# Taking the softmax sums from the context matmuls' 65th row, and dropping drains, in a four-stage model on eight cores

## The chip, the cores and the metric

The kernel runs on all 8 cores of one Trainium2 chip. Each core works on one of the 8 batch rows, 2048 tokens of 1024 values, and no core talks to another. The time is that of the slowest core, in microseconds (us) of the device. A core has TensorE (PE), VectorE (DVE), ScalarE (ACT), GpSimd (POOL) and SyncE (SP), each with a queue that it works through in order; PE writes to PSUM, and weights are loaded into it by instructions of their own (PEld).

## What is computed

Two layers, each an attention part and a feed-forward part with a layer norm behind: a gated recurrence, a ternary feed-forward, an attention with relative positions, and a two-deep local-attention block. The change is mainly in the third:

```python
# 8 x 2048 tokens, 16 heads of 64, R = 64
dist = jnp.clip(idx[None, :] - idx[:, None], -R, R) + R
pe_k = rel_emb_k[dist]
pe_v = rel_emb_v[dist]
score = jnp.einsum('bhqd,bhkd->bhqk', q, k) + jnp.einsum('bhqd,qkd->bhqk', q, pe_k)
attn = jax.nn.softmax(score, axis=-1)
ctx = jnp.einsum('bhqk,bhkd->bhqd', attn, v) + jnp.einsum('bhqk,qkd->bhqd', attn, pe_v)
ctx = jnp.transpose(ctx, (0, 2, 1, 3)).reshape(b, s, d)
x = _layernorm(x + ctx @ W_out + b_out)
```

Beyond a distance of 64 all keys on one side share one row of `rel_emb_v`, so their part of the second sum is that row times the sum of their attention weights. That is why the kernel needs two partial sums for every query: that over the keys far to the left and that over the keys far to the right.

The fourth part (two layers, 8 heads, windows of 512) has an attention over 1024 keys for each window and divides by the softmax's sum in the same way.

## The kernel before

The program is written as one list of instructions for each engine, with semaphores: `p.op(engine, ...)` appends an operation, `p.wait(engine, semaphore, value)` a wait, and `p.drain(engine)` an instruction that lets the engine's own earlier work finish. The order in these lists is written out by hand, and each engine keeps to it. The stages run one after the other: build_load_x, build_block0, build_block1, build_block2, build_block3, build_output_store.

build_block2 is the attention with relative positions. For each of 16 heads (`h`) it first writes query products to memory (L947 to L953, 16 transfers), and then goes through 4 query blocks (`qb`) of 512 queries. I call one of these 64 passes a block. A block has these parts:

- Opening: L979 and L981, two matmuls with one row of zeros as weights, open two rows of sums in PSUM, `pb[0:1, 0:512]` and `pb[0:1, 1536:2048]`.
- 16 key steps (`kt`) of 128 keys. The scores come from up to three kinds of matmul: right of the diagonal band (L1050), in the band (L1044 transposes of loaded products, L1055), and left of it (L1060). The exponent (L1067) is taken by ScalarE for all 512 queries. L1072 multiplies the exponents with the 64 values and a column of ones (`VE[kt]`, 65 columns) into `ctxA`, rows 0 to 63 the context and row 64 the full sum. L1075 and L1078 multiply the far parts of the exponents with one column of ones (`onesbc`), into the two rows of sums. The scores of step kt wait for the exponent of step kt - 2 only; the context matmul waits for that of its own step.
- Closing of the two rows (L1079, L1081), and the part for near keys: transposes, a trip through memory, transposes back, 16 small matmuls into `ctxA` (L1101 to L1153).
- Tail: ScalarE copies the two rows of sums to SBUF (L1160, L1161), TensorE adds their products with the two rows of `rel_emb_v` to `ctxA` (L1165, L1167) and closes it (L1169, token `a_close`). VectorE takes the reciprocal of row 64 (L1173) and rounds it (L1175), TensorE spreads it over 64 partitions (L1177), VectorE copies the context (L1181) and multiplies (L1186, token `hb_tok`). TensorE waits for `hb_tok` before the next block.

build_block3 has, in each of two layers, 32 passes over heads and windows. A pass makes scores for a maximum (L1673, L1678, L1682), sends it through memory (L1688 and two transfers into row 64 of the queries), runs the tail of the pass before (attn_tail: L1606, then L1611, L1613, L1615, L1617, L1621, L1627), and then opens and fills its own scores (L1704, L1716, L1727). Three loops in the stages take squares and sum them by turns of VectorE and TensorE, 64 times each: L841 with L847, L1449 with L1455, L1801 with L1807.

## Time and profile before

| | |
|---|---|
| median of 2 runs (lowest, highest) | 11150.66 us (11142.19, 11159.12) |
| profiled execution | 11150.62 us |
| its span, slowest core (fastest core) | 11149.1 us (10966.6 us) |
| busy, PE / PEld | 5631.9 / 1996.6 us |
| busy, DVE / ACT / POOL | 2748.6 / 1682.2 / 840.8 us |
| mean granted clock of the slowest core | 0.608 |

The span is from the first to the last instruction of a core. Busy times of the engines overlap, so they say what an engine did and not what the time waited for; the chain of work that ended last says that. The granted clock is TensorE's, as a share of full speed (2.4 GHz). Ends of matmuls are modelled, so the distance from one start to the next is the safer measure of what a matmul takes.

### The profile page before, as it was taken

Reading aid. Unit: us, or ns where it says so; the run is one execution under the profiler, and the core shown is the slowest. Engines: PE = TensorE matmul, PEld = TensorE weight load, DVE = VectorE, ACT = ScalarE, POOL = GpSimd, SP = SyncE. Lnnn points to the kernel's source line nnn. Section 1 sums busy time; section 2 is a strip of 40 time slices with the busy share of each in tenths; the row PEclk is TensorE's granted clock in tenths of the full one; section 3 lists DMA queues with packets and bytes.
Section 4 is the critical chain, followed back from the end, with each engine's and each line's share of the span. In section 5 each row is a group of like instructions: output and inputs, shape, how many; then the busy total and the mean of one; then the engine's idle time right before and its main releaser. Section 6 shows DMA issues by size and latency. Waiting matters only on the chain.

```text
span 11149.1 us, 60408 instructions; the slowest of 8 cores (10966.6 to 11149.1 us)
## 1 busy us (share of the span) xinstructions
PE 5631.9 (51%) x19111; PEld 1996.6 (18%) x19111; DVE 2748.6 (25%) x4041; ACT 1682.2 (15%) x3009; POOL 840.8 (8%) x813
## 2 busy tenths in 40 slices
PE   4344444444545544545554546323445962344694
PEld 2111111111111111111111112101112420111241
DVE  5655220000000000000000001263344116333314
ACT  1100102222222222222222221001110100111100
POOL 0000100000000000000000000021111102111010
PEclk7676775555555555555555556655567975556796
DMA  3000221111110111111001111200002320000231
GB/s 53 9 4 0 53 31 33 31 32 35 32 32 22 32 32 35 32 35 32 28 25 32 32 35 46 48 5 0 1 0 22 35 28 0 1 0 5 22 35 60
DMA packets 458427, 285.29 MB, mean 26 GB/s; under 512 B 307482, under 2 KB 403995, under 8 KB 454027
## 3 DMA queue, kind: packets, MB, share of 16 engines
q0 software_dynamic: 222240, 81.89, 6.5%
q1 hardware_dynamic: 162156, 103.56, 3.5%
q10 hardware_dynamic: 73728, 95.98, 2.4%
q8 instruction: 169, 2.77, 0.1%
q14 instruction: 134, 1.10, 0.1%
HBM read 227.39 MB, written 118.96 MB: 31 GB/s over the span
## 4 chain that ended last, share of the span: by engine, by line
PE 44%; DVE 17%; DMA 16%; ACT 12%; issue 6%; SPq 2%; DVEq 1%; POOL 1%; ACTq 1%; POOLq 0%; PEldq 0%
DMA sc_amax<-amaxc 6%; PE pm L1072 6%; ACT xb L1067 6%; DMA sc_qre<-wm 4%; PE pm L1905 3%; PE pb L1926 3%; PE pm L1050 2%; SPq L49 2%; PE pb L1075 2%; PE pm L1060 2%; PE pb L1078 2%; DVE wm L1173 2%; DMA xb<-sc_e 2%; PE pm L1044 2%; PE pm L1420 2%
## 5 line engine op out<-in xcount | busy, mean ns | idle before, releaser
L1173 DVE RECIPROCAL wm<-pm 1x512 f32<-1x512 f32 x64 | 214.5, 3352 | 4738.8 <-PE pm L1169 4738.8
L1067 ACT ACTIVATE xb<-pm 128x512 bf16<-128x512 f32 x1024 | 611.4, 597 | 2554.9 <-PE pm L1060 1665.8
L1072 PE MATMUL pm<-xb,U 128*65 128x512 bf16 x576 | 349.9, 608 | 488.9 <-ACT xb L1067 488.9
L49 POOL DMA_DIRECT2D wj<-sc_qre x128 | 70.5, 553 | 5013.1 <-PE pm L1055 2631.1
L947 PE MATMUL pb<-wj 128*128 128x512 bf16 x256 | 147.2, 588 | 500.4 <-ACT wm L953 446.1
L1138 PE MATMUL pb<-identb,xb 128*128 128x128 bf16 x1024 | 119.4, 309 | 539.2 <-DMA xb<-sc_e 539.2
L1682 DVE TENSOR_REDUCE amaxc<-pm 128x1 f32<-128x640 f32 (+4 forms) x256 | 181.8, 740 | 686.3 <-PE pm L1678 684.6
L1727 ACT ACTIVATE xb<-pb 128x512 bf16<-128x512 f32 x448 | 244.7, 595 | 547.8 <-PE pb L1716 547.3
L1060 PE MATMUL pm<-wj 128*128 128x512 bf16 (+4 forms) x576 | 301.5, 524 | 0.0
L1050 PE MATMUL pm<-qer,wj 128*128 128x512 bf16 (+4 forms) x576 | 299.6, 520 | 0.0
L1078 PE MATMUL pb<-xb,onesbc 128*1 128x512 bf16 (+4 forms) x576 | 287.5, 499 | 0.0
L220 PE MATMUL pm<-xb,wj 128*128 128x512 bf16 x512 | 141.2, 444 | 282.4 <-ACT U L231 260.0
L1075 PE MATMUL pb<-xb,onesbc 128*1 128x512 bf16 (+4 forms) x576 | 282.9, 491 | 0.0
L1072 PE MATMUL pm<-xb 128*65 128x512 bf16 x256 | 155.6, 608 | 215.4 <-ACT xb L1067 215.4
L1704 PE MATMUL pb<-wm,zbuf 1*65 1x512 bf16 x64 | 38.6, 603 | 438.3 <-DMA wj<-sc_amax 436.0
L953 ACT ACTIVATE wm<-pb 128x512 f32<-128x512 f32 x256 | 152.9, 597 | 670.3 <-DMA sc_qre<-wm 499.5
L1905 PE MATMUL pm<-xb,wm 128*128 128x512 bf16 (+1 forms) x704 | 188.4, 392 | 99.4 <-DVE xin L1853 99.4
L1420 PE MATMUL pm<-xb,wm 128*128 128x512 bf16 x384 | 109.4, 411 | 220.6 <-DVE xin L1391 169.9
L1145 ACT ACTIVATE xb<-pb 128x512 bf16<-128x512 bf16 x256 | 132.2, 602 | 553.6 <-PE pb L1138 553.6
L1613 DVE RECIPROCAL wm<-wm 1x512 f32<-1x512 f32 x64 | 213.8, 3341 | 5.1 <-issue 0.4
L1072 PEld LDWEIGHTS pm<-xb,U 128*65 128x65 bf16 x576 | 74.9, 130 | 751.3 <-issue 751.3
L49 POOL DMA_DIRECT2D wm<-l1f_w x152 | 128.1, 850 | 1028.5 <-PE pm L1905 521.5
(433 smaller groups left out, 9420.5 us busy)
## 6 DMA issues: line engine op xcount, KB each, us to landing
sc_qre<-wm ACTq DMA_DIRECT2D x256, 256.0 KB, 2.0
wm<-l1f_w POOLq DMA_DIRECT2D x116, 256.0 KB, 4.2
sc_xspill<-xr SPq DMA_DIRECT2D x16, 1024.0 KB, 13.9
xb<-sc_e SPq DMA_DIRECT2D x128, 128.0 KB, 2.8
xb<-sc_e ACTq DMA_DIRECT2D x128, 128.0 KB, 2.9
wm<-W_qkv POOLq DMA_DIRECT2D x48, 256.0 KB, 4.2
sc_e<-xb ACTq DMA_DIRECT2D x112, 96.0 KB, 2.0
sc_e<-xb SPq DMA_DIRECT2D x112, 96.0 KB, 1.9
```

The lines of the kernel that those rows point to most:

```text
L49: self.on(eng, lambda q, o=out, i=in_, s=sem: q.dma_start(out=o, in_=i).then_inc(s.h, 16))
L1050: q.matmul(o, l, r, start=s1, stop=s2), s_tr)
L1060: q.matmul(o, l, r, start=s1, stop=s2), s_tr)
L1067: q.activation(out=o, in_=i_, func=AF.Exp), s_se)
L1072: q.matmul(o, l, r, start=st, stop=False), s_tr)
L1075: q.matmul(o, onesbc[:], r, start=False, stop=False), s_tr)
L1078: q.matmul(o, onesbc[:], r, start=False, stop=False), s_tr)
L1173: p.op("vector", lambda q: q.reciprocal(out=srow[0:1, 0:512], in_=ctxA[64:65, 0:512]))
L1420: q.matmul(o, l, r, start=st, stop=sp),
L1727: q.activation(out=o, in_=i_, func=AF.Exp), s_se)
L1905: q.matmul(o, l, r, start=st, stop=sp),
L1926: q.matmul(o, l, r, start=st, stop=sp),
```

## The change

In build_block2, L1072, L1075 and L1078 are replaced by up to three matmuls with the 65 columns of `VE[kt]`, each over its part of the 512 queries: far right keys into `ctxC` (a bank of `pb`), the band into `ctxA`, far left keys into `ctxB` (a bank of `pm`). All three tiles are opened with zeros at the start of a block. The sums of the far parts are now row 64 of `ctxB` and `ctxC`. The tail adds three tiles instead of reading one: three operations on the sums before the reciprocal, and for the context a copy on ScalarE and two adds on VectorE before the multiplication. The wait of TensorE for the copy of the block before (`cc_prev`) is dropped.

In build_block3 the copy of the sums before the reciprocal (L1611) is dropped; the reciprocal reads PSUM.

In both, drains of VectorE are dropped in several places: L840, L1388, L1394, L1448, L1520, L1764, L1787, L1800, L1931 and L1976.

```diff
@@ -837,7 +837,6 @@
     for (base, ps) in ((0, pm), (8, pb)):
         for nb in range(NB):
             for dt in range(NDT):
-                p.drain("vector")
                 p.op("vector", lambda q, d=dt, b=base, n=nb: q.tensor_tensor(
                     out=bfull[:, 0:512], in0=qkT[b + d][:, n * 512:(n + 1) * 512],
                     in1=qkT[b + d][:, n * 512:(n + 1) * 512], op=OP.mult), s_ve)
@@ -974,12 +973,10 @@
             qb0 = qb * 512
             p.wait("tensor", s_qe[par], qe_tok)
             ctxA = pm[0:66, 1024:1536]
-            if cc_prev:
-                p.wait("tensor", s_ve, cc_prev)
-            p.op("tensor", lambda q: q.matmul(pb[0:1, 0:512], zbuf[0:1, 0:1], MQS[0:1, 0:512],
-                                              start=True, stop=False), None)
-            p.op("tensor", lambda q: q.matmul(pb[0:1, 1536:2048], zbuf[0:1, 0:1], MQS[0:1, 0:512],
-                                              start=True, stop=False), None)
+            ctxB = pm[0:66, 1536:2048]
+            ctxC = pb[0:66, 0:512]
+            for ctx in (ctxA, ctxB, ctxC):
+                p.op("tensor", lambda q, o=ctx: q.matmul(o, zbuf[0:1, 0:66], MQS[0:1, 0:512], start=True, stop=False), None)
             tchunks = {}
             tlist = []
             for kt in range(NTT):
@@ -1067,19 +1064,20 @@
                      q.activation(out=o, in_=i_, func=AF.Exp), s_se)
                 prev_exp_tok[pp] = p.sems["s_se"].n
                 p.wait("tensor", s_se, prev_exp_tok[pp])
-                p.op("tensor", lambda q, o=ctxA[0:65, 0:512], l=VE[kt][:, 65 * h:65 * h + 65],
-                     r=a_sl(kt, 0, 512), st=(kt == 0):
-                     q.matmul(o, l, r, start=st, stop=False), s_tr)
+                if Rs > qb0:
+                    p.op("tensor", lambda q, o=ctxC[0:65, 0:Rs - qb0], l=VE[kt][:, 65 * h:65 * h + 65],
+                         r=a_sl(kt, 0, Rs - qb0):
+                         q.matmul(o, l, r, start=False, stop=False), s_tr)
+                if b0 < b1:
+                    p.op("tensor", lambda q, o=ctxA[0:65, b0 - qb0:b1 - qb0], l=VE[kt][:, 65 * h:65 * h + 65],
+                         r=a_sl(kt, b0 - qb0, b1 - qb0):
+                         q.matmul(o, l, r, start=False, stop=False), s_tr)
                 if Ls < qb0 + 512:
-                    p.op("tensor", lambda q, o=pb[0:1, Ls - qb0:512], r=a_sl(kt, Ls - qb0, 512):
-                         q.matmul(o, onesbc[:], r, start=False, stop=False), s_tr)
-                if Rs > qb0:
-                    p.op("tensor", lambda q, o=pb[0:1, 1536:1536 + Rs - qb0], r=a_sl(kt, 0, Rs - qb0):
-                         q.matmul(o, onesbc[:], r, start=False, stop=False), s_tr)
-            p.op("tensor", lambda q: q.matmul(pb[0:1, 0:512], zbuf[0:1, 0:1], MQS[0:1, 0:512],
-                                              start=False, stop=True), None)
-            p.op("tensor", lambda q: q.matmul(pb[0:1, 1536:2048], zbuf[0:1, 0:1], MQS[0:1, 0:512],
-                                              start=False, stop=True), s_tr)
+                    p.op("tensor", lambda q, o=ctxB[0:65, Ls - qb0:512], l=VE[kt][:, 65 * h:65 * h + 65],
+                         r=a_sl(kt, Ls - qb0, 512):
+                         q.matmul(o, l, r, start=False, stop=False), s_tr)
+            p.op("tensor", lambda q, o=ctxB: q.matmul(o, zbuf[0:1, 0:66], MQS[0:1, 0:512], start=False, stop=True), None)
+            p.op("tensor", lambda q, o=ctxC: q.matmul(o, zbuf[0:1, 0:66], MQS[0:1, 0:512], start=False, stop=True), s_tr)
             bc_close = p.sems["s_tr"].n
             pchunk = [pb[:, 512:1024].bitcast(BF16), pb[:, 1024:1536].bitcast(BF16)]
 
@@ -1157,31 +1155,45 @@
             p.op("tensor", lambda q: q.nop(), s_tr)
             pv_done = p.sems["s_tr"].n
             p.wait("scalar", s_tr, pv_done)
-            p.op("scalar", lambda q: q.activation(out=sab[0:1, 0:512], in_=pb[0:1, 0:512], func=AF.Copy), None)
+            p.op("scalar", lambda q: q.activation(out=sab[0:1, 0:512], in_=ctxB[64:65, 0:512], func=AF.Copy), None)
             p.op("scalar", lambda q: q.activation(out=sab[0:1, 512:1024],
-                                                  in_=pb[0:1, 1536:2048], func=AF.Copy), s_se)
+                                                  in_=ctxC[64:65, 0:512], func=AF.Copy), s_se)
             sat_tok = p.sems["s_se"].n
             p.wait("tensor", s_se, sat_tok)
             p.op("tensor", lambda q: q.matmul(ctxA[0:64, 0:512], pvb[0:1, 0:64], sab[0:1, 0:512],
                                               start=False, stop=False), None)
             p.op("tensor", lambda q: q.matmul(ctxA[0:64, 0:512], pvb2[0:1, 0:64], sab[0:1, 512:1024],
                                               start=False, stop=False), None)
-            p.op("tensor", lambda q, o=ctxA[0:65, 0:512]: q.matmul(o, zbuf[0:1, 0:65], MQS[0:1, 0:512], start=False, stop=True), s_tr)
+            p.op("tensor", lambda q, o=ctxA: q.matmul(o, zbuf[0:1, 0:66], MQS[0:1, 0:512], start=False, stop=True), s_tr)
             a_close = p.sems["s_tr"].n
             p.wait("vector", s_tr, a_close)
             p.drain("vector")
-            p.op("vector", lambda q: q.reciprocal(out=srow[0:1, 0:512], in_=ctxA[64:65, 0:512]))
+            p.op("vector", lambda q: q.tensor_copy(out=srow[0:1, 0:512], in_=ctxA[64:65, 0:512]))
+            p.drain("vector")
+            p.op("vector", lambda q: q.tensor_tensor(out=srow[0:1, 0:512], in0=srow[0:1, 0:512],
+                                                     in1=ctxB[64:65, 0:512], op=OP.add))
+            p.drain("vector")
+            p.op("vector", lambda q: q.tensor_tensor(out=srow[0:1, 0:512], in0=srow[0:1, 0:512],
+                                                     in1=ctxC[64:65, 0:512], op=OP.add))
+            p.drain("vector")
+            p.op("vector", lambda q: q.reciprocal(out=srow[0:1, 0:512], in_=srow[0:1, 0:512]))
             p.drain("vector")
             rb_tok = p.op("vector", lambda q: q.tensor_copy(out=rbrow[:], in_=srow[0:1, 0:512]), s_ve)
             p.wait("tensor", s_ve, rb_tok)
             p.op("tensor", lambda q: q.matmul(pb[0:64, 1536:2048], onesbr[0:1, 0:64], rbrow[:],
                                               start=True, stop=True), s_tr)
             rbc_tok = p.sems["s_tr"].n
+            p.wait("scalar", s_tr, a_close)
+            p.op("scalar", lambda q: q.activation(out=ccf[:, 0:512], in_=ctxC[0:64, 0:512], func=AF.Copy), s_se)
+            cc_tok = p.sems["s_se"].n
+            p.wait("vector", s_se, cc_tok)
+            p.wait("vector", s_tr, rbc_tok)
             p.drain("vector")
-            cc_tok = p.op("vector", lambda q: q.tensor_copy(out=ccf[:, 0:512],
-                                                            in_=ctxA[0:64, 0:512]), s_ve)
-            cc_prev = cc_tok
-            p.wait("vector", s_tr, rbc_tok)
+            p.op("vector", lambda q: q.tensor_tensor(out=ccf[:, 0:512], in0=ccf[:, 0:512],
+                                                     in1=ctxA[0:64, 0:512], op=OP.add))
+            p.drain("vector")
+            p.op("vector", lambda q: q.tensor_tensor(out=ccf[:, 0:512], in0=ccf[:, 0:512],
+                                                     in1=ctxB[0:64, 0:512], op=OP.add))
             p.drain("vector")
             hb_tok = p.op("vector", lambda q, hh=h, b0=qb0: q.tensor_tensor(
                 out=hb[hh // 2][64 * (hh % 2):64 * (hh % 2) + 64, b0:b0 + 512],
...
@@ -1445,7 +1455,6 @@
         for (b0, ps) in ((0, pm), (4, pb)):
             for nb in range(NB):
                 for dt in range(4):
-                    p.drain("vector")
                     p.op("vector", lambda q, d=dt, b=b0, n=nb: q.tensor_tensor(
                         out=bfull[:, 0:512], in0=QKV[b + d][:, n * 512:(n + 1) * 512],
                         in1=QKV[b + d][:, n * 512:(n + 1) * 512], op=OP.mult), s_ve)
...
@@ -1608,9 +1616,7 @@
             st["av"] = p.sems["s_tr"].n
             p.wait("vector", s_tr, st["av"])
             p.drain("vector")
-            p.op("vector", lambda q: q.tensor_copy(out=ccrow, in_=pb[64:65, 0:512]))
-            p.drain("vector")
-            p.op("vector", lambda q: q.reciprocal(out=ccrow, in_=ccrow))
+            p.op("vector", lambda q: q.reciprocal(out=ccrow, in_=pb[64:65, 0:512]))
             p.drain("vector")
             rb = p.op("vector", lambda q: q.tensor_copy(out=rbrow3, in_=ccrow), s_ve)
             p.wait("tensor", s_ve, rb)
...
@@ -1797,7 +1801,6 @@
                      s_tr if j == 7 else None)
         for j in range(8):
             for nb in range(NB):
-                p.drain("vector")
                 p.op("vector", lambda q, jj=j, n=nb: q.tensor_tensor(
                     out=bfull[:, 0:512], in0=hsh[jj][:, n * 512:(n + 1) * 512],
                     in1=hsh[jj][:, n * 512:(n + 1) * 512], op=OP.mult), s_ve)
```

The drains of the other lines are removed in the same way.

## Rows read from the trace of the kernel before

**Rows 1.** The chain that ended last: shares of the span by engine (the page).
```profile
PE 44%; DVE 17%; DMA 16%; ACT 12%; issue 6%; SPq 2%; DVEq 1%; POOL 1%; ACTq 1%; POOLq 0%; PEldq 0%
```

**Rows 2.** Windows, build_block2's blocks: length, PE, PEld, DVE, ACT, POOL busy, clock, DMA.
```profile
1814.00:6820.00 5006.00, 2522.01 (x7708) 799.88 (x7708) 356.45 (x301) 1042.26 (x1878) 149.92 (x279) 0.50 0.10 31
```

**Rows 3.** Timeline, one step without a band: start, us, engine, line, form [idle before].
```profile
3048.08 0.61 PE L1072 MATMUL pm<-xb,U 128*65 128x512 bf16 x1 [0.84 <-ACT xb L1067]
3048.62 0.58 PE L1078 MATMUL pb<-xb,onesbc 128*1 128x512 bf16 x1
3049.13 0.10 PEld L1050 LDWEIGHTS pm<-qer,wj 128*128 128x128 bf16 x1 [0.44 <-issue]
3049.14 0.61 PE L1050 MATMUL pm<-qer,wj 128*128 128x512 bf16 x1
...
3050.58 0.61 PE L1072 MATMUL pm<-xb,U 128*65 128x512 bf16 x1 [0.84 <-ACT xb L1067]
```

**Rows 4.** Groups by line and form, build_block2: count, busy us, mean ns, idle before.
```profile
L1078 PE MATMUL pb<-xb,onesbc 128*1 128x512 bf16 x336 | 196.3, 584 | 0.0
...
L1078 PE MATMUL pb<-xb,onesbc 128*1 128x320 bf16 x64 | 27.2, 425 | 0.0
...
L1078 PE MATMUL pb<-xb,onesbc 128*1 128x448 bf16 x48 | 25.5, 531 | 0.0
```

**Rows 5.** Timeline, one step with a band in three pieces.
```profile
3035.74 0.26 PE L1050 MATMUL pm<-qer,wj 128*128 128x64 bf16 x1
3035.74 0.15 PEld L1055 LDWEIGHTS pm<-wj 65*128 65x128 bf16 x1
...
3036.47 0.60 ACT L1067 ACTIVATE xb<-pm 128x512 bf16<-128x512 f32 x1 [2.25 <-PE pm L1060]
...
3037.75 0.32 PE L1075 MATMUL pb<-xb,onesbc 128*1 128x192 bf16 x1
...
3037.86 0.26 PE L1078 MATMUL pb<-xb,onesbc 128*1 128x64 bf16 x1
...
3038.05 0.47 PE L1044 MATMUL pm<-identf,wm 128*128 128x128 f32 x1
```

**Rows 6.** Timeline, block 3: the opening of a pass and its first scores.
```profile
7869.80 0.60 PE L1704 MATMUL pb<-wm,zbuf 1*65 1x512 bf16 x1 [7.88 <-DMA wj<-sc_amax]
7870.33 0.13 PEld L1716 LDWEIGHTS pb<-wj,vex 128*128 128x128 bf16 x2 [0.44 <-issue]
7870.34 1.03 PE L1716 MATMUL pb<-wj,vex 128*128 128x512 bf16 x2
```

**Rows 7.** Timeline, the tail of a block of build_block2.
```profile
3090.90 0.63 PE L1165 MATMUL pm<-wm,pvb 1*64 1x512 bf16 x1
...
3091.33 0.63 PE L1167 MATMUL pm<-wm,pvb 1*64 1x512 bf16 x1
...
3096.61 0.68 DVE L1181 COPY wm<-pm 64x512 f32<-64x512 f32 x1
...
3096.66 0.60 PE L1177 MATMUL pb<-wm,onesbr 1*64 1x512 bf16 x1 [4.14 <-DVE wm L1175]
3097.42 0.68 DVE L1186 TENSOR_TENSOR hb<-wm,pb 64x512 bf16<-64x512 f32 x1
```

**Rows 8.** Waits of TensorE: us in total, times, longest.
```profile
PE pb L1704 <- DMA wj<-sc_amax: 436.0, 63, 16.0
...
PE pm L1044 <- DMA wm<-sc_qre: 96.3, 16, 7.8
...
PE pb L979 <- DVE hb L1186: 58.1, 48, 1.6
```

**Rows 9.** Timeline, block 3: the copy of the sums and the reciprocal.
```profile
7856.59 0.69 DVE L1611 COPY wm<-pb 1x512 f32<-1x512 f32 x1
...
7857.35 3.34 DVE L1613 RECIPROCAL wm<-wm 1x512 f32<-1x512 f32 x1
```

**Rows 10.** Source line 2050 (a layer norm's row): durations in ns, least, median, most.
```profile
L2050 DVE TENSOR_TENSOR U<-pm,U x4: 2279/2279/2279, 758.0 to 11019.3; 1x2048 f32<-1x2048 f32 x4
```

More of the change, by code:

```diff
@@ L1519, in build_block3 @@
                     p.wait("vector", s_ge, prev_s)
-                p.drain("vector")
                 for blk in range(4):
@@ L1610, in attn_tail @@
             p.drain("vector")
-            p.op("vector", lambda q: q.tensor_copy(out=ccrow, in_=pb[64:65, 0:512]))
-            p.drain("vector")
-            p.op("vector", lambda q: q.reciprocal(out=ccrow, in_=ccrow))
+            p.op("vector", lambda q: q.reciprocal(out=ccrow, in_=pb[64:65, 0:512]))
             p.drain("vector")
@@ L1763, in build_block3 @@
             p.wait("vector", s_tr, womm_last)
-            p.drain("vector")
             for nb in range(NB):
@@ L1786, in build_block3 @@
                  s_ve if j == 3 else None)
-            p.drain("vector")
         h2v = p.sems["s_ve"].n
@@ L1799, in build_block3 @@
             for nb in range(NB):
-                p.drain("vector")
                 p.op("vector", lambda q, jj=j, n=nb: q.tensor_tensor(
@@ L1930, in build_block3 @@
             p.wait("vector", s_se, prevge)
-            p.drain("vector")
             if k < 20:
@@ L1975, in build_block3 @@
             p.wait("vector", s_tr, w2mm[do])
-            p.drain("vector")
             for nb in range(NB):
```

## Prediction

> **What bounds the kernel now.** I read the page's chain of work by line first: no single engine bounds the kernel, the chain hops between TensorE (44%), VectorE (17%), DMA (16%) and ScalarE (12%) [rows 1]. Much of it lies in the third stage, build_block2, the attention with relative positions. The windows view shows it from 1814 to 6820 us: 5006 of 11149 us, with a granted clock of 0.50 of full speed throughout, which is the lower level, 1.2 GHz [rows 2]. The stage is 16 heads x 4 query blocks of 512 = 64 blocks, each with 16 key steps of 128 keys, so 1024 steps.
>
> The timeline of one step shows why it is a chain and not a pipeline. The context matmul L1072 starts at 3048.08, the ones matmul L1078 at 3048.62, the next scores L1050 at 3049.14, and the next context matmul at 3050.58: 2.50 us for a step [rows 3]. L1072 waits for the exponent of its own step, and the next scores are queued on TensorE behind the ones matmul. So scores, exponent, context matmul and ones matmul lie end to end, and whatever leaves TensorE's queue there comes off the time in full.
>
> **The ones matmuls that go.** Of each step the keys far to the left and far to the right of a query had a ones matmul (L1075, L1078) for their sums; now the 512 columns are split at the same borders into three PSUM tiles whose 65th row is that sum. The columns of the context matmul stay 512 in all. A step without a diagonal part (one full ones matmul) goes from two matmuls to one. A step with a diagonal part has as many pieces as it had matmuls. What a removed one costs is its start to the next start: 0.52 us at 512 columns [rows 3], against a busy time of 0.584; the same 0.065 off the busy times of the narrower forms gives 0.36 at 320 and 0.47 at 448 columns [rows 4]. A 192 and a 64 in one step take 3037.75 to 3038.05, 0.30 us together [rows 5]. Each count in [rows 4] stands twice, for L1078 and for its mirror image L1075: 672 steps have 512 columns, 128 have 320, 96 have 448, and the other 128 have the pair.
> 672 x 0.52 + 128 x 0.36 + 96 x 0.47 + 128 x 0.30 = 349 + 46 + 45 + 38 = 479 us off.
>
> **The weight load behind the context matmul.** From L1072 to L1078 are 0.54 us, and L1078's weights are loaded only when the stream is over: the load row says 0.44 idle, then L1050's says the same [rows 3]. In the same trace weights are loaded under a running matmul where both have the same shape in the array: L1055's load starts with the L1050 matmul (both use more than 64 rows and columns), and in block 3 two L1716 matmuls, with a satisfied wait between them, take 1.03 us together, so 0.43 from start to start when the second lasts 0.60 [rows 5, 6]. The load after L1704 (1 row) had to wait, 0.44 idle again [rows 6]. Now the context pieces (65 columns) and the next scores (128) follow each other with no 1-column matmul between. So I take 0.43 for the context interval in place of 0.54. Splitting costs next to nothing: scores of 64+256+192 columns start at 3035.74 and the exponent at 3036.47, 0.73 us, where one piece of 512 needs 0.70 [rows 3, 5]. 1024 x 0.11 - 128 x 0.03 = 109 us off; bounds 0 and 113.
> The Trainium skill (TensorEngine Tiling (Array Packing), Key Properties) says that a change of tiling mode, not just of tile, drains TensorE. The load rows agree; by the rule this term is 109, without it 0.
>
> **Opening and closing.** Three opening matmuls of 66 columns stand where two of 1 column did. Two like these (L1165, L1167) start 0.43 apart [rows 7]. In 48 of 64 blocks TensorE had waited for VectorE before the opening, so it is on the path; in the 16 first blocks of a head TensorE then waits 96.3 / 16 = 6.0 us for a transfer anyway and hides it [rows 8]. 48 x 0.43 = 21 us on. The two closings stay two: nothing, or 0.05 x 64 = 3.
>
> **The tail of a block.** Sums now lie in three tiles, so VectorE has three 1x512 operations before the reciprocal. The copy is the one block 3 has: 0.69, and 0.07 to the reciprocal behind a drain [rows 9]. The adds are not in this trace in that shape; nearest is L1186, a two-input operation of 512 columns with one operand in PSUM, 0.68 [rows 7]. 0.76 + 2 x (0.68 + 0.08) = 2.28 us a block. Behind the reciprocal the copy L1181 ran beside the broadcast L1177, and L1186 started at 3097.42, when both were done [rows 7]. Now the copy is ScalarE's, waiting for a_close and done under the reciprocal (3.34 [rows 9]); only the next block's exponents are queued behind it, and those need TensorE first. But two adds of 64x512 stand between the broadcast's end (3097.26, plus 0.22 for two waits and the drain) and the multiplication: 3097.48 + 2 x (0.68 + 0.10) = 3099.04, which is 1.62 later. TensorE's next block waits for that multiplication, so all is exposed: (2.28 + 1.62) x 64 = 249 us on. Bounds: a subtraction of 1x2048 with one operand in PSUM took 2.28 [rows 10], a quarter is 0.57, so 4 x 0.11 x 64 = 28 less; up to 11 more if each gap is 0.13 as between L1181 and L1186.
>
> **Block 3 and the drains.** The copy L1611 goes, 0.69 + 0.07 in 64 places. It is covered: behind it the next block's L1704 waits for a transfer, 63 times of 64 [rows 8], and in [rows 6, 9] the copy began at 7856.59; with its 0.69, the reciprocal's 3.34 and three more operations of at most 0.7 the tail is over by about 7863, and L1704 starts at 7869.80. Only the last block of each of the two layers has no such cover: 2 us off. Were the transfer gone it would be worth 0.76 x 64 = 49. Of the removed drains 192 lie in loops where VectorE and TensorE alternate (L840, L1448, L1800). L1186 started 0.16 after L1177's end with a drain in that gap [rows 7], so one is worth 0 to 0.16; I take 0.05: 10 us off, bounds 0 and 30. The other removed ones stand beside longer work.
>
> **Sum.** -479 - 109 + 21 + 249 - 2 - 10 = -330 us. The profiled execution took 11150.6 (span 11149.1), the median of the runs is 11150.66, so both give 10821 us. The main case's own range: all low ends, 479 + 113 + 2 + 30 - 21 - 221 = 382 off, 10769; all high ends, 479 + 109 + 2 - 24 - 260 = 306 off, 10845.
>
> **Rivals.**
> *The weight load stays exposed.* The context interval stays 0.54 because the wait between it and the next scores holds the load back: 109 is lost, 10930. The satisfied wait between two L1716 speaks against it [rows 6]. Chance 0.08.
> *Every piece pays its own load.* 672 steps at 0.54, 224 with two pieces at 0.65, 128 with three at 0.76 make 606 us where 553 were: 53 more instead of 109 less, 10983. L1055's load under L1050 speaks against it [rows 5]. Chance 0.05.
> The Trainium skill (TensorE: Matmul & The Clock Gate, Part 3) has a rule for this rival: weight loads overlap a running matmul only when the row group differs. L1050 and L1055 share their rows and overlap, so the trace does not bear it out.
> *The tail eats the gain (slower).* If VectorE's four adds, with partition 64 of PSUM beside partition 0 of SBUF, cost what the reciprocal does, 3.34 in place of 0.68, the tail grows by 4 x 2.66 x 64 = 681: 11502. It decides from 330 / 256 = 1.29 us more per add, 1.97 each. The 1x2048 subtraction, 2.28 for four times the length, speaks against it [rows 10]. Chance 0.03.
> *The clock rises.* If the denser stage were granted 2.4 GHz, scores and context streams would halve, 0.43 to 0.21 twice a step: 1024 x 0.44 = 450 more off, 10371. The mean over 5006 us is 0.50 [rows 2], so it never rose, and nothing in the rows says that it would. Chance 0.02.
> *The sum holds:* 0.80; 0.02 are left for what I don't see.
>
> **How the numbers follow.** Predicted is the main case, 10821 us. The range, 10765 to 10935, takes in the main case and the first rival, 0.88, less a margin for the spread of runs; the likeliest case's own is 10769 to 10845. Faster by over 2% means below 10928, and 2% is about what a measurement of this kernel can tell from no change: main case 0.80, clock 0.02 and a part of the first rival: 0.85. Within 2%: the rest of the first rival, the second, and some of the unseen: 0.12. Slower: 0.03.
>
> **What would show it.** In the timeline of a step without a diagonal part: L1072's successor followed at 0.43 by the scores, whose load starts with the context matmul, and 1.87 us from step to step. The 1x512 and 64x512 adds near 0.68, and 3.9 us more from a_close to the next opening. Block 3's L1704 still ended by the transfer and its stage as long as before. Clock 0.50 in the stage. Wrong if the load row of the scores still shows 0.44 idle, if adds are over 1 us, or if a new wait appears before the first scores of a block.

## The result, and the profile after

The changed kernel takes 10813.3 us (median of 11 executions, 10671.39 to 10896.74), the kernel before 11137.76 us beside it (10 executions, 11055.55 to 11189.87). The ratio is 0.968, 95% interval 0.9636 to 0.9724: 3.2% faster. In some executions one half of the cores runs a per cent or more longer at a lower granted clock; the medians here and below are of all executions, the ratios and their intervals leave these out, and so a ratio is not the quotient of the medians beside it. Predicted were 10821 us, in 10765 to 10935. The profiled execution of the changed kernel took 10788.22 us. Its page begins with the span, then the busy time of each engine, and further down the chain of work that ended last, by engine:

```profile
span 10786.7 us, 59401 instructions; the slowest of 8 cores (10691.9 to 10786.7 us)
...
PE 5050.2 (47%) x18503; PEld 1982.2 (18%) x18503; DVE 2880.2 (27%) x4233; ACT 1720.5 (16%) x3073; POOL 839.7 (8%) x813
...
PE 40%; DVE 19%; DMA 17%; ACT 12%; issue 6%; SPq 2%; DVEq 1%; POOL 1%; ACTq 1%; POOLq 0%; PEldq 0%
```

TensorE is busy 582 us less than before and VectorE 132 us more, and in the chain TensorE's share fell from 44% to 40% while VectorE's rose from 17% to 19% [rows 1]: matmuls left, and VectorE got new work in the tail. The windows view of the attention stage (stretch, length, then busy time and count of PE, PEld, DVE, ACT and POOL, the granted clock, DMA share, GB/s) still says 0.50, the 1.2 GHz level of [rows 2]:

```profile
1810.00:6490.00 4680.00, 1974.99 (x7109) 791.52 (x7109) 522.61 (x550) 1079.88 (x1941) 149.91 (x279) 0.50 0.11 33
```

**What I compare.** Whole times of this kernel scatter by about 1%, more than some of the terms. So I measure the stage by itself: from the start of the first opening matmul to the end of the last multiplication. The source-line view gives both (durations least, median and most in ns, first and last start in us); here core 7 before, then core 7 after:

```profile
L979 PE MATMUL pb<-xin,zbuf x64: 577/579/582, 1745.9 to 6753.7; 1*1 1x512 bf16 x64
...
L1186 DVE TENSOR_TENSOR hb<-wm,pb x64: 678/680/681, 1818.8 to 6819.6; 64x512 bf16<-64x512 f32 x64
```

```profile
L979 PE MATMUL pm<-xin,zbuf x128: 601/615/629, 1752.7 to 6450.6; 1*66 1x512 bf16 x128
...
L1198 DVE TENSOR_TENSOR hb<-wm,pb x64: 679/680/682, 1820.3 to 6511.1; 64x512 bf16<-64x512 f32 x64
```

Before: 6819.6 + 0.7 - 1745.9 = 5074.4 us. After: 6511.1 + 0.7 - 1752.7 = 4759.1. The medians over the eight cores are 5064.3 and 4744.8; core by core the stage is 314 to 322.5 us shorter, median 319. The terms of the prediction that lie in the stage (-479, -109, +21, +249) came to -318. Below, "stage" is this median over the cores unless a core is named. The kernel before has one profile, so the stages of all experiments are held against that one execution; from one execution to the next the same stage differs by 3 to 8 us (5064.3 here, 5069.0 in the run below that leaves the stage alone).

The timeline of a step without a band (start, length, engine, line, form, idle time before and what ended it), to be held beside [rows 3]:

```profile
2959.89 0.61 PE L1070 MATMUL pb<-xb,U 128*65 128x512 bf16 x1 [0.84 <-ACT xb L1064]
2959.99 0.10 PEld L1047 LDWEIGHTS pm<-qer,wj 128*128 128x128 bf16 x1
2960.29 0.63 PE L1047 MATMUL pm<-qer,wj 128*128 128x512 bf16 x1
2961.02 0.60 ACT L1064 ACTIVATE xb<-pm 128x512 bf16<-128x512 f32 x1 [1.28 <-PE pm L1047]
2961.76 0.61 PE L1070 MATMUL pb<-xb,U 128*65 128x512 bf16 x1 [0.84 <-ACT xb L1064]
```

A step takes 1.87 us where it took 2.50. The ones matmul is gone, and the weights of the scores are loaded 0.10 us after the context matmul began, with no idle time in the load's row.

The tail of a block and the next opening:

```profile
2996.78 0.63 PE L1167 MATMUL pm<-xin,zbuf 1*66 1x512 bf16 x1
...
2997.51 0.59 ACT L1187 ACTIVATE wm<-pb 64x512 f32<-64x512 f32 x1 [2.28 <-PE pm L1167]
...
2997.57 0.69 DVE L1171 COPY wm<-pm 1x512 f32<-1x512 f32 x1 [101.41 <-PE pm L1167]
...
2999.08 0.68 DVE L1176 TENSOR_TENSOR wm<-wm,pb 1x512 f32<-1x512 f32 x1
...
2999.84 3.34 DVE L1179 RECIPROCAL wm<-wm 1x512 f32<-1x512 f32 x1
...
3003.81 0.60 PE L1183 MATMUL pb<-wm,onesbr 1*64 1x512 bf16 x1 [6.40 <-DVE wm L1181]
...
3004.57 0.68 DVE L1192 TENSOR_TENSOR wm<-wm,pm 64x512 f32<-64x512 f32 x1 [0.90 <-PE pb L1183]
...
3005.32 0.68 DVE L1195 TENSOR_TENSOR wm<-wm,pm 64x512 f32<-64x512 f32 x1
...
3006.07 0.68 DVE L1198 TENSOR_TENSOR hb<-wm,pb 64x512 bf16<-64x512 f32 x1
...
3007.01 1.03 PE L979 MATMUL pm<-xin,zbuf 1*66 1x512 bf16 x2 [2.60 <-DVE hb L1198]
...
3008.39 0.61 PE L1057 MATMUL pm<-wj 128*128 128x512 bf16 x1
```

From the closing matmul to the next opening are 3007.01 - 2996.78 = 10.23 us. The same stretch before, core 7, around [rows 7]:

```profile
3091.89 0.63 PE L1169 MATMUL pm<-xin,zbuf 1*65 1x512 bf16 x1
...
3098.46 0.58 PE L979 MATMUL pb<-xin,zbuf 1*1 1x512 bf16 x1 [1.20 <-DVE hb L1186]
...
3099.40 0.61 PE L1060 MATMUL pm<-wj 128*128 128x512 bf16 x1
```

That was 3098.46 - 3091.89 = 6.57 us. All four adds take 0.68 us, on one partition or on 64.

**The stage in parts.** I added up the starts of these instructions over all 64 blocks, on each core before and after, and took the median of the differences over the cores (lowest and highest in brackets):

| part | us |
|---|---|
| opening: first opening matmul to the first matmul behind the openings, 48 blocks within a head | +22 (21 to 22) |
| the same, first blocks of the 16 heads | +5 (2 to 8) |
| the 16 steps: from there to the first closing of the sums | -587 (-588 to -587) |
| the two closings, up to the next transpose | +3 (3 to 3) |
| part for near keys, up to the last closing matmul | +1 (-1 to 8) |
| tail: last closing matmul to the multiplication | +242 (242 to 243) |
| multiplication to the next opening, 48 blocks within a head | -5 (-5 to -5) |
| multiplication to the next head's opening, 15 times | 0 (-5 to 3) |

The wait of TensorE for block 3's transfer after, on core 3 (us in total, times, longest), for [rows 8]:

```profile
PE pb L1710 <- DMA wj<-sc_amax: 492.6, 64, 15.3
```

### The profile page after: what moved, and what is told of

Read it like the earlier page. It is cut to its first block, busy times and chain, and to the rows that moved or that the text cites. A ratio compares the mean times of both kernels' runs of the same rounds, so it can differ in the third digit from the quotient of the medians.

```text
span 10786.7 us, 59401 instructions; the slowest of 8 cores (10691.9 to 10786.7 us)
## 1 busy us (share of the span) xinstructions
PE 5050.2 (47%) x18503; PEld 1982.2 (18%) x18503; DVE 2880.2 (27%) x4233; ACT 1720.5 (16%) x3073; POOL 839.7 (8%) x813
## 4 chain that ended last, share of the span: by engine, by line
PE 40%; DVE 19%; DMA 17%; ACT 12%; issue 6%; SPq 2%; DVEq 1%; POOL 1%; ACTq 1%; POOLq 0%; PEldq 0%
DMA sc_amax<-amaxc 6%; ACT xb L1064 6%; DMA sc_qre<-wm 5%; PE pm L1908 3%; PE pb L1929 3%; PE pb L1070 3%; PE pm L1078 2%; SPq L49 2%; DVE wm L1179 2%; PE pm L1047 2%; DMA xb<-sc_e 2%; PE pm L1057 2%; PE pm L1430 2%; PE pb L1722 1%; PE pm L1974 1%
## 5 line engine op out<-in xcount | busy, mean ns | idle before, releaser
L1171 DVE COPY wm<-pm 1x512 f32<-1x512 f32 x64 | 43.8, 685 | 4170.6 <-PE pm L1167 4170.6
L1078 PE MATMUL pm<-xb,U 128*65 128x512 bf16 (+2 forms) x448 | 245.4, 548 | 258.3 <-ACT xb L1064 258.3
L1619 DVE RECIPROCAL wm<-pb 1x512 f32<-1x512 f32 x64 | 214.5, 3352 | 229.7 <-PE pb L1614 228.6
L1183 PE MATMUL pb<-wm,onesbr 1*64 1x512 bf16 x64 | 38.4, 601 | 410.8 <-DVE wm L1181 410.8
L1908 PE MATMUL pm<-xb,wm 128*128 128x512 bf16 (+1 forms) x704 | 182.5, 382 | 99.8 <-DVE xin L1856 99.8
L1136 PEld LDWEIGHTS pb<-identb,xb 128*128 128x128 bf16 x1024 | 104.2, 143 | 552.2 <-issue 552.2
L1151 PE MATMUL pm<-xb,xin 128*64 128x128 bf16 x1024 | 120.7, 312 | 147.9 <-ACT xb L1143 147.9
```

What stands on the lines that cost most here:

```text
L1078: q.matmul(o, l, r, start=False, stop=False), s_tr)
L1136: q.matmul(o, i_, idb[:], is_transpose=True, start=True, stop=True),
L1908: q.matmul(o, l, r, start=st, stop=sp),
```

## Experiments

Theory M is the sum of the prediction. The rivals differ from run to run and stand in the expectations.

### The attention part alone

```diff
 build_block2: as in the changed kernel (three context tiles, no ones matmuls, new tail)
 build_block3 and all dropped drains outside build_block2: as before
```

> Only the part in build_block2 (three context tiles, new tail); all drains and block 3's copy stay as before. The stage is read from the first opening matmul to the end of the last multiplication: over the eight cores its median was 5064 us before and 4745 us in the changed kernel. My theory: the whole gain is here, the stage is 4745 again (within 5), the step without a band 1.87 us, and the time is about 318 us below before, ratio 0.971. Rival, that the dropped drains and the dropped copy carry a good part of the gain: the stage would be longer or the ratio above 0.975.

Measured: 10903.87 us (median of 4) against 11230.14 us (13), ratio 0.9721, interval 0.967 to 0.9771. Stage 4753.1 us, 311 less than before and 8 more than in the changed kernel, where within 5 were expected; the run of the next section, which leaves the stage alone and was profiled on the same chip as this one, has 5069.0, 316 more. The steps are 587 us shorter than before and the tail 243 longer, as in the changed kernel. The squares loop of build_block2 kept its 82.3 us. So the gain is that of build_block2.

### The rest alone

```diff
 build_block2: as before
-                p.drain("vector")          (L840, L1388, L1394, L1448, L1520 and five more)
-            p.op("vector", lambda q: q.tensor_copy(out=ccrow, in_=pb[64:65, 0:512]))
```

> Only the dropped drains and the dropped copy L1611 in block 3; attention as before. My theory: the squares loop of build_block2 (64 turns) falls from 82.4 us to about 79.8, the two others by as much together twice, block 3's first scores still wait for the transfer, the attention stage stays 5064: 10 us in all, ratio 0.999, no difference that can be measured. Rival, that the copy was exposed in the 64 passes: another 49 us, ratio about 0.994.

Measured: 11205.14 us against 11230.14 us, ratio 0.9999, interval 0.9961 to 1.0037: the same. Stage 5069.0 us. On its slowest core all 64 passes still wait for the transfer (59 to 64 on the eight cores):

```profile
PE pb L1697 <- DMA wj<-sc_amax: 471.3, 64, 17.3
```

The squares loop of build_block2 went from 82.3 us to 79.5 to 79.8. In the source-line view, core 3 after and core 7 before, a turn of VectorE and TensorE is (1663.5 - 1583.7) / 63 = 1.267 us where it was 1.308:

```profile
L840 DVE TENSOR_TENSOR bfull<-xr x64: 425/427/453, 1583.7 to 1663.5; 128x512 bf16<-128x512 bf16 x64
```

```profile
L841 DVE TENSOR_TENSOR bfull<-xr x64: 424/424/426, 1585.2 to 1667.6; 128x512 bf16<-128x512 bf16 x64
```

So a drain between two engines that take turns cost 0.04 us, 2.6 us for 64, and some 8 us for the three loops, an estimate that takes the first loop's turn for all: far below what a comparison of whole times can show.

### The ones matmuls with the context's weights

The kernel before keeps its ones matmuls, but with the 65 columns of `VE[kt]` as weights, so that no 1-column matmul is left between 65- and 128-column ones.

```diff
-                         q.matmul(o, onesbc[:], r, start=False, stop=False), s_tr)
+                         q.matmul(o, VE[kt][:, 65 * h:65 * h + 65], r, start=False, stop=False), s_tr)
 (o = 65 rows of the same bank; openings and closings with 65 columns too; sums read from row 64)
```

> The kernel before, with one thing changed: the ones matmuls use the 65 columns of VE as weights in place of the single column of ones (outputs are 65 rows, the sum is row 64). Number of matmuls and streamed columns stay. My theory, that a change of the number of weight columns from over 64 to 1 and back keeps the next weight load from running under the stream: both changes go, the context interval falls from 0.54 to 0.43 and the ones interval from 0.52 to 0.43, the step from 2.50 to about 2.30, the stage by 1024 x 0.2 = 200 us to about 4865. Rival, that the load is held back by the wait before the scores or by the row group being the same: step 2.50, stage 5064. A second rival, that 65-column loads cost more: stage up by 1152 x 0.05 = 58 us.

Measured: stage 4873.3 us, 191 less than before (one execution, 11025.27 us). No arithmetic was removed; each of the 512-column matmuls only became wider. Core 3, one step:

```profile
3008.51 0.61 PE L1072 MATMUL pm<-xb,U 128*65 128x512 bf16 x1 [0.84 <-ACT xb L1067]
...
3008.91 0.63 PE L1078 MATMUL pb<-xb,U 128*65 128x512 bf16 x1
...
3009.34 0.63 PE L1050 MATMUL pm<-qer,wj 128*128 128x512 bf16 x1
...
3010.81 0.61 PE L1072 MATMUL pm<-xb,U 128*65 128x512 bf16 x1 [0.84 <-ACT xb L1067]
```

The intervals are 0.40 and 0.43 us instead of 0.54 and 0.52 [rows 3], 2.30 us a step instead of 2.50. The steps of all blocks are 203 us shorter than before, where 200 were expected. Of the 587 us that the steps gave in the changed kernel, then, about a third is not the ones matmuls' streaming but the weight loads beside a 1-column matmul. It is the change between the two widths that costs, and not the one column by itself: in the kernel before, a 1-column load behind a 1-column matmul does not wait (the second ones matmul of [rows 5] starts 0.11 us after the first, which has 192 columns), and two openings with 1-column weights start 0.38 us apart (L979 at 3098.46, L981 at 3098.84).

### The adds ahead of the broadcast's wait

```diff
             p.wait("vector", s_se, cc_tok)
-            p.wait("vector", s_tr, rbc_tok)
             ... the two adds of 64x512 ...
+            p.wait("vector", s_tr, rbc_tok)
             p.drain("vector")
```

This is the changed kernel with the two adds beside the broadcast instead of behind it.

> The changed kernel with VectorE's wait for the broadcast matmul moved from before the two context adds to behind them, before the multiplication. The adds need only the closing of the tiles and ScalarE's copy. My theory: VectorE was idle 0.90 us there in each block, and the adds (0.68 each) fill it: the multiplication starts 0.73 us earlier, 64 x 0.73 = 47 us, stage 4698. [...]

Measured: stage 4698.6 us, 46 less than the changed kernel and 54 less than the attention part alone, which was profiled on the same chip (one execution, 10826.06 us). Core 7, from the rounding of the reciprocal on:

```profile
3000.08 0.41 DVE L1181 CAST wm<-wm 1x512 bf16<-1x512 f32 x1
...
3000.58 0.68 DVE L1191 TENSOR_TENSOR wm<-wm,pm 64x512 f32<-64x512 f32 x1
...
3000.64 0.60 PE L1183 MATMUL pb<-wm,onesbr 1*64 1x512 bf16 x1 [6.40 <-DVE wm L1181]
...
3002.09 0.68 DVE L1198 TENSOR_TENSOR hb<-wm,pb 64x512 bf16<-64x512 f32 x1
```

The multiplication starts 2.01 us after the rounding did, where it took 2.82 in the changed kernel (its timeline has the broadcast's add at 3004.57 and the rounding at 3003.25, so 3006.07 - 3003.25): 0.81 us, where 0.73 was expected, and 64 x 0.81 = 52. Added up over the blocks the tail is 52 us shorter on every core; what is missing to it in the 46 lies mostly in the part for near keys, which varies from one execution to another. So the tail lies on the path in every block, as the prediction had it. The adds take 0.68 us beside the broadcast's matmul as they did behind it: neither it nor ScalarE's copy holds them back.

### The context matmuls one step later: the changed kernel

Now the other half of the argument: that the removed matmuls counted in full because scores, exponent and context lie end to end. If the context matmul of a step is issued behind the scores of the next step, that is no longer so.

```diff
+                def ctx_mm(...):      # the wait for the step's exponent and its context matmuls
+                    ...
+                if held:
+                    held.pop()()      # the step before, behind this step's scores
+                held.append(ctx_mm)
+            held.pop()()
```

> The changed kernel with the context matmuls of a step issued behind the scores of the next step (the exponents have a tile for each step and the scores two, so nothing else changes). My theory, that the steps cost what lies end to end in them: the exponent now runs beside TensorE, a step without a band costs TensorE's two intervals, 2 x 0.43 = 0.86 us, in place of 1.87. About 0.9 x 1024 = 920 us off the stage, about 3830 us, if the clock stays at 0.50; ratio to the kernel before about 0.89. If the denser stream is granted the full clock, ScalarE's 0.60 plus its gap bounds the step at about 0.7, 150 us less still. Rival, that the step is held by something outside TensorE's order (the semaphore's way to ScalarE and back): less than half of the 920.

Measured: 9632.56 us (5) against 11172.72 us (7), ratio 0.8602, interval 0.8549 to 0.8655. The stage takes 3518 us. That is 312 us below the 3830 expected for a clock of 0.50, and 160 below what was expected with the full clock. Core 7, the exponents, and the windows of the stage:

```profile
3004.83 1.20 ACT L1065 ACTIVATE xb<-pm 128x512 bf16<-128x512 f32 x2 [0.23 <-PE pm L1058]
...
3006.26 1.20 ACT L1065 ACTIVATE xb<-pm 128x512 bf16<-128x512 f32 x2 [0.23 <-PE pm L1058]
```

```profile
1800.00:5260.00 3460.00, 1505.44 (x7105) 695.03 (x7103) 514.71 (x542) 1067.27 (x1941) 149.93 (x279) 0.62 0.15 44
```

Two exponents now take 3006.26 - 3004.83 = 1.43 us from pair to pair, 0.715 us a step. And the granted clock is no longer 0.50: it is 0.62 in the mean of the stage. Context and scores start 0.40 apart early in the block, before 3004.5, and 0.21 to 0.22 apart behind it, as on the same core:

```profile
3005.57 0.38 PE L1080 MATMUL pm<-xb,U 128*65 128x512 bf16 x1 [0.23 <-ACT xb L1065]
3005.78 0.38 PE L1058 MATMUL pm<-wj 128*128 128x512 bf16 x1
```

ScalarE does not set this step alone, for it waits 0.23 us for scores in each pair. What sets it is a chain over two steps, because the scores are queued behind the context matmul of an earlier exponent: that exponent from 3004.83 to 3005.43, its context matmul at 3005.57, the scores at 3005.78, their exponent at 3006.26, or 0.60 + 0.14 + 0.21 + 0.48 = 1.43 us. Whether a hold of two steps would break this chain was not tried.

How much of the gain is the order's and how much the clock's can be estimated. At the lower clock a step of this kernel takes 0.93 us (below), so the order alone is worth 1024 x (1.87 - 0.93) = 963 us, more than the 920 of my theory; the stage fell by 4744.8 - 3518.1 = 1227. The other 264 went with the higher clock, an estimate that takes every step for one without a band.

### The same order in the kernel before

The same `ctx_mm`, holding L1072, L1075 and L1078 of the kernel before.

> The kernel before with the same reordering (context and ones matmuls of a step behind the next step's scores). At a clock of 0.50 a step costs TensorE 0.54 + 0.52 + 0.43 = 1.49 us, the stage about 4080 to 4150, and the change would still be worth its 318 us on top of this order. Rival: with the denser stream the full clock is granted or ScalarE bounds the step, the ones matmuls are hidden, and the change, whose tail costs 249 us more a stage, is worth little or turns into a loss.

Measured: 9633.91 us, ratio 0.8607 (0.8532 to 0.8682). Stage 3564.4 us. It lies 516 to 586 us below the 4080 to 4150 that were expected for a clock of 0.50. Under this order the change to three tiles is worth 46 us in the stage and nothing that the whole time shows (9632.56 against 9633.91). My theory, that it would keep its gain, fell, and the rival held. Core 5, at both levels of the clock:

```profile
3016.32 0.61 PE L1061 MATMUL pm<-wj 128*128 128x512 bf16 x1
3016.72 0.63 PE L1074 MATMUL pm<-xb,U 128*65 128x512 bf16 x1
3017.28 0.58 PE L1077 MATMUL pb<-xb,onesbc 128*1 128x512 bf16 x1
3017.80 0.61 PE L1061 MATMUL pm<-wj 128*128 128x512 bf16 x1
...
3023.74 0.39 PE L1061 MATMUL pm<-wj 128*128 128x512 bf16 x1
3024.04 0.38 PE L1074 MATMUL pm<-xb,U 128*65 128x512 bf16 x1
3024.35 0.38 PE L1077 MATMUL pb<-xb,onesbc 128*1 128x512 bf16 x1
3024.66 0.39 PE L1061 MATMUL pm<-wj 128*128 128x512 bf16 x1
```

TensorE runs without a gap: 1.48 us a step at 1.2 GHz, 0.92 us at 2.4 GHz (windows of the stage: 0.64). With three tiles, on core 7 of the late order of the changed kernel, the context matmuls start at 3001.00, 3001.83 and 3002.87 at the lower clock, 0.93 us a step, and every 0.715 us later. So at the lower clock the removed matmul is worth 0.55 us a step, 563 us for 1024, and at the higher 0.205, 210 us, against a longer tail and opening. The 46 us lie between the two: added up over the blocks, the steps are 303 us shorter with three tiles than with the ones matmuls (587 in the serial order), the tail is 242 longer and the openings 22. Why it came out so much smaller than 319: the denser order brings the clock up, and at that clock the matmul is cheap; the tail, which is VectorE's, is not.

### Both orders together, and the wide weights in the late order

With the adds ahead of the wait as well:

> late_ctx and early_adds together, as the version that should beat both. The moved wait gave 46 us in the serial kernel; the tail of a block is the same in both orders, so another 46 us below late_ctx, stage about 3785 or 46 below what late_ctx shows.

Measured: 9513.73 us, ratio 0.8527 (0.8491 to 0.8562), stage 3471.7 us, 46 below the kernel with late context matmuls: the adds' gain is the same in both orders.

If the tail is what the three tiles cost and the 1-column weights are what the two-row form costs, the best should be the kernel before with the late order and 65-column weights, which has neither:

> wide_ones and before_late together: the kernel before, with context and ones matmuls of a step behind the next step's scores, and 65 weight columns for the ones matmuls too. It streams up to 1024 columns a step for context and sums where the changed kernel streams 512, but keeps the short tail. In late_ctx a step without a band took 0.93 us at half clock and 0.71 at the full clock, where ScalarE bounds it; in before_late 1.48 and 0.92. My theory, that under this order the extra columns are mostly hidden and the tail is what the two differ by: at the full clock three intervals of 0.22 fit under ScalarE's 0.71; at half clock a step costs 3 x 0.43 = 1.29, 0.36 more than late_ctx in some 6 of 16 steps of a block, 64 x 6 x 0.36 = 138 us; the tail and the opening cost 249 + 21 less. Stage 3518 + 138 - 270 = about 3386 us, below late_early's 3472, ratio to the kernel before about 0.845. Rival, that the ones matmuls stay exposed at the full clock as well: stage near before_late's 3564 less the weight loads, about 3500.

Measured: 9522.42 us (5 executions, 9354.26 to 9705.43), the kernel before beside it 11135.1 us; stage 3374.3 us, expected 3386 (the theory behind that number held only in part, see below). Its executions scattered too far to rank it, so I ran it again with the one that it has to beat, on one chip:

> late_wide again, beside late_early on one chip, since the two were timed on different chips and their whole times overlap (9354 to 9705 and 9510 to 9667). In its stage it was 98 us shorter (3374 against 3472), and outside the stage the two differ by the dropped drains and copy alone, about 10 us the other way. Expected: some 90 us below late_early in the medians, if the runs' spread from block 3's transfers lets it be seen.

> late_early again, the partner of late_wide_b: about 90 us above it. If the tail were not what the two differ by, the two would be equal in their medians and in their stages.

Measured: late order with 65-column weights 9478.61 us against 11165.0 us, ratio 0.8483 (0.8446 to 0.8521), stage 3377.4 us; late order with three tiles and early adds 9546.69 us, ratio 0.8544 (0.8505 to 0.8583), stage 3464.9 us. In the stages the first is 87.5 us ahead: its steps are 119 us longer, its tail 191 and its openings 20 shorter. The medians of the whole stand 68 us apart, and three of the first one's four executions (9458 to 9483; the fourth 9527) lie below all four of the other (9520 to 9550), but the two intervals of the ratios overlap, so that order of the whole times is likely and not settled. Windows of the first (core 3) and a stretch of it at the higher clock:

```profile
1800.00:5100.00 3300.00, 1614.49 (x7590) 717.69 (x7588) 346.05 (x293) 1022.95 (x1852) 149.92 (x279) 0.64 0.15 46
```

```profile
3052.19 0.38 PE L1074 MATMUL pm<-xb 128*65 128x512 bf16 x1
3052.40 0.38 PE L1080 MATMUL pb<-xb 128*65 128x512 bf16 x1
3052.62 0.38 PE L1051 MATMUL pm<-qer,wj 128*128 128x512 bf16 x1
...
3053.83 0.38 PE L1074 MATMUL pm<-xb 128*65 128x512 bf16 x1
```

The context matmul, the ones matmul and the scores start 0.21 and 0.22 apart, with no price for a change of shape; behind the scores TensorE waits for the exponent. Two steps take 3053.83 - 3052.19 = 1.64 us, 0.82 a step: less than the 0.92 with 1-column weights, more than the 0.715 with three tiles. So my theory that the extra columns are hidden at the full clock was wrong: the extra matmul lies in the chain over two steps, 1.43 + 0.21 = 1.64. That the stage came out 12 us from the expectation is in part luck, since the steps cost 119 us more than in the late order of the changed kernel, where I had put 138, all at the lower clock and none at the higher. It is the fastest kernel of the study, 1687 us less in the stage than the kernel before, and it does not have the change.

## Why the prediction was right, point by point

**What bounds the stage.** The step is a chain on TensorE and ScalarE, and what leaves TensorE's queue in it comes off in full: 2.50 to 1.87 us, as forecast. The late orders show the condition of that sentence: with the chain taken apart, the same change is worth 46 us in the stage.

**The ones matmuls, -479.** Not separable from the next term in the changed kernel; both together gave -587 in the steps where -588 were forecast. The run with the wide weights shows the intervals: 0.52 us of such a matmul is 0.40 to 0.43 of it and 0.09 to 0.11 that its narrow weights cost.

**The weight load, -109.** The load now starts 0.10 us behind the context matmul's start, and 0.40 us lie between the starts of the two matmuls, where I took 0.43; in return the exponent starts 0.73 us after the scores instead of 0.70, so the step is the 1.87 us that I had. Where the next instruction is not one of 128 rows, the load still waits; the changed kernel, core 3, at a transpose of 64 rows behind a context matmul:

```profile
3013.64 0.61 PE L1078 MATMUL pm<-xb,U 128*65 128x512 bf16 x1 [0.84 <-ACT xb L1064]
3014.17 0.18 PEld L1041 LDWEIGHTS pm<-identf,wj 64*128 64x128 f32 x1 [0.44 <-issue]
```

There are 48 + 48 such places, with transposes of 64 rows, and 64 closings (1 row): 160 x 0.11 = 18 us, which this term overlooked because it treated all 1024 successors alike. As the steps came to -587 all the same, those with a band must have given back about as much elsewhere; where was not traced. The agreement of the sum to 1 us is luck to that extent.

The Trainium skill (TensorEngine Tiling (Array Packing), Key Properties) says that a change of tiling mode drains TensorE. The load rows of the kernel before, of the changed kernel and of the one with wide weights fit that, with 0.09 to 0.11 us beside a 1-column matmul at 1.2 GHz, if matmuls of 1 and of 65 or 128 columns count as different modes; that they do is inferred from these rows.

**Opening, +21.** The scores start 3008.39 - 3007.01 = 1.38 us after the first opening. In the kernel before, behind the block of [rows 7], the first opening starts at 3098.46 and the scores at 3099.40, 0.94 us: 0.44 x 48 = 21. In the first blocks of the heads, where I had it all hidden behind a transfer, the opening grew by 5 us in total, and the closings by 3.

**The tail, +249.** From the closing matmul to the multiplication it came to +242 us (9.30 us a block where it was 5.53), and the next opening follows 0.10 us sooner behind the multiplication in the 48 blocks within a head, -5: +237 together, within the bounds of 221 to 260. The operations were sized rightly (0.69, 0.68); three gaps were not. Between drained adds lie 0.07 us where I took 0.10 (3005.32 + 0.68 = 6.00 to 3006.07); from the broadcast's end to the add 3004.57 - 3004.41 = 0.16, where I took 0.22; and from the multiplication's end to the opening 3007.01 - 3006.75 = 0.26, where before it was 3098.46 - 3098.10 = 0.36. ScalarE's copy, 2997.51 to 2998.10, was over long before the adds, as forecast.

**Block 3's copy, -2.** The wait for the transfer ends 64 passes after on the slowest core (61 to 64 on the eight), and the whole is the same with this part alone. Covered, as argued.

**The drains, -10.** 64 x 0.04 x 3 = 8 us, the first loop's measurement taken for all three; I took 0.05 each.

**The rivals.** That the load stays exposed, that every piece pays one and that the adds cost over 1 us are each excluded by a row above. That the clock rises did not happen in the changed kernel. It was given 0.02 because nothing in the rows spoke for it; the late orders show that a stage of this kind can reach the higher level, in an order with fewer gaps on TensorE; the change alone leaves the wait of 0.84 us in every step.

**A near miss is partly luck.** In the stage the tail came out 12 us below its term, and the openings and closings 8 above theirs, so that the errors cancel. The profiled spans differ by 11149.1 - 10786.7 = 362 us, not by 319 and 8, the medians by 324, and the ratio of 0.968 stands for 0.032 x 11137.76 = 356 (10821 of 11150.66 is 0.9704, inside its interval). That 10813.3 lies 8 us from the forecast is therefore no measure of how good the sum was; the stage is. The rest is not the change's. The kernel before, core 0, waits for block 3's small transfers

```profile
PE pb L1704 <- DMA wj<-sc_amax: 257.3, 53, 12.9
```

where core 7 waits 436.0 us [rows 8]. That is 179 of the 182.5 us by which the two cores' spans differed. Such differences go with pairs of cores and with the execution; any whole time holds up to 180 us of them.

## What to carry over

Ask first whether the work of one step lies end to end: if it does, each matmul removed counts from start to start, and each operation added to the tail too. But then try the order first: issuing the scores of the next step ahead of the context of this one was worth 14% of the whole time, four times this change, and left next to nothing for it. A matmul whose weights have one column is hardly cheaper here than one with 65 (0.38 us from start to start against 0.40 to 0.43, both at 1.2 GHz); beside wider ones it costs more (0.52 to 0.54), and padding its weights to its neighbours' width removes that.

## What the runs showed of the hardware that I had not expected

- **The clock followed the order of the work.** In the stage it was 0.50 throughout before and after, with the engine idle 0.84 us before each context matmul; in the late orders, where these gaps were shorter or gone, it rose within a block (0.82 from 3020 to 3024 and 1.00 from 3024 to 3028 us on core 5 of the late order of the kernel before, TensorE busy throughout and without a gap from 3016.32 on) and was 0.61 to 0.65 in the mean of the stage. Some 260 us of the late context's gain went with it (the estimate above). That the gaps are what held it down is argued from this; no run varied the gaps alone.
- **A change of shape has a price at the higher clock too.** At 2.4 GHz a 1-column matmul and its 65- and 128-column neighbours start 0.30 to 0.31 us apart, equal shapes 0.21 to 0.22.
- **Wait times for one small transfer per pass differ by core.** 257 us on core 0 and 436 on core 7 in the same execution and the same program, in pairs of neighbouring cores. What decides it was not tried.
